# Alignment and feed-forward on one core: the tokens loaded once as tiles of 128 in a row, and their statistics moved between quadrants by small matmuls

## The reference, cut to what matters

```python
x = x + align(ctx_1024, layernorm(x))        # x (8, 512, 256), ctx (8, 64, 256), all float32
x = x + ffn(layernorm(x), w1, b1, w2, b2)    # 256 -> 1024 -> 256, quantised to 8 bits
# align, for each of the 8 batches, small = ctx (64 rows), large = tokens (512 rows):
D = sqrt(max(|a|^2 + |b|^2 - 2 a.b, 0))                        # 64 x 512
R[i, j] = D[i, j] + min(R[i-1, j], R[i, j-1], R[i-1, j-1])     # dynamic time warping
# backtrack the cheapest path from (63, 511) to (0, 0); expanded[j] += small[i] on the path
# ffn: h = relu(quant(quant(x) @ quant(w1).T + quant(b1))); out = quant(h) @ quant(w2).T + quant(b2)
```

## Time and profile before

| | us |
|---|---|
| median of 3 runs (205.34 to 207.87) | 205.64 |
| profiled execution, whole | 205.88 |
| its span, first to last instruction | 204.1 |
| first `to_chunks` starts | 44.16 |
| busy DVE / PE / ACT / POOL | 154.2 / 105.5 / 99.4 / 20.1 |

### The profile page before, as it was taken

How to read it: one execution, slowest core, us unless ns; L and a number is a source line. 1 busy time by engine, 2 the same in 40 slices (tenths; PEclk the granted TensorE clock), 3 DMA queues, 4 the chain that set the end, 5 groups by cost and what they waited for, 6 DMA issues and landing times.

```text
span 204.1 us, 3699 instructions
## 1 busy us (share of the span) xinstructions
PE 105.5 (52%) x1219; PEld 70.3 (34%) x1219; DVE 154.2 (76%) x743; ACT 99.4 (49%) x169; POOL 20.1 (10%) x81
## 2 busy tenths in 40 slices
PE   0089199100070000000000856699999999997993
PEld 0078199100040000000000322266565656564672
DVE  0566823999999999999999188586969696967342
ACT  0567039699992000021440005767576758566740
POOL 6455832300000000000000000000000000000000
PEclk9999859955555555555555699999999999999999
DMA  5999301999500000001103321001111113030214
GB/s 165 230 230 234 71 3 19 351 360 348 166 5 0 0 2 0 0 0 66 64 0 115 62 37 19 0 3 51 51 56 51 67 41 103 0 108 4 99 64 141
DMA packets 20597, 17.28 MB, mean 85 GB/s; under 512 B 6369, under 2 KB 20194, under 8 KB 20450
## 3 DMA queue, kind: packets, MB, share of 16 engines
q1 hardware_dynamic: 17986, 15.71, 26.5%
q10 hardware_dynamic: 2592, 1.34, 3.1%
HBM read 11.54 MB, written 5.51 MB: 84 GB/s over the span
## 4 chain that ended last, share of the span: by engine, by line
DVE 56%; PE 22%; ACT 10%; issue 6%; DMA 3%; SPq 1%; DVEq 0%; ACTq 0%
DVE Y L916 5%; DVE R L745 5%; PE y L1065 5%; ACT h_int L566 5%; DVE Dm L865 4%; PE h L1051 4%; DVE stats L848 4%; DVE X L843 4%; DMA X<-in_x_dram 3%; ACT M L560 3%; DVE A L713 3%; DVE enter L903 3%; DVE bcarry L902 3%; PE e L983 3%; DVE carry L733 3%
## 5 line engine op out<-in xcount | busy, mean ns | idle before, releaser
L566 ACT ACTIVATE h_int<-h,b_s 128x512 int16<-128x512 f32 x64 | 43.0, 685 | 8.6 <-PE h L1051 7.7
L1051 PE MATMUL h<-M,w1T 128*128 128x512 bf16 x128 | 37.9, 381 | 2.5 <-ACT h_int L566 1.7
L1065 PE MATMUL y<-w2T,XT 128*128 128x256 bf16 x256 | 37.7, 273 | 0.3 <-DVE XT L878 0.3
L1078 PE MATMUL y<-w1T 128*128 128x512 bf16 x19 | 5.9, 463 | 51.6 <-DVE S_lo L930 51.6
L1065 PEld LDWEIGHTS y<-w2T,XT 128*128 128x128 bf16 x256 | 25.0, 98 | 12.4 <-DVE XT L878 0.5
L878 DVE TENSOR_SCALAR XT<-h_int 128x1024 bf16<-128x1024 int16 x32 | 13.2, 424 | 18.3 <-ACT h_int L566 18.3
L1078 PEld LDWEIGHTS y<-w1T 128*128 128x128 bf16 x19 | 2.0, 116 | 54.6 <-DVE S_lo L930 51.9
L572 ACT ACTIVATE code<-Y,shifts 128x640 bf16<-128x640 bf16 x3 | 2.5, 828 | 37.5 <-DVE enter L903 37.5
L1020 PE MATMUL t<-ident_bf,w_raw 128*128 128x128 bf16 x32 | 4.6, 311 | 20.4 <-ACT w_raw L530 19.2
L689 DVE BATCH_NORM_STATS2 stats<-X 128x6 f32<-128x256 f32 x32 | 10.8, 410 | 4.1 <-DMA X<-in_x_dram 4.1
L843 DVE TENSOR_TENSOR X<-e,X 128x512 f32<-128x512 f32 x16 | 10.2, 682 | 4.6 <-PE e L1031 4.6
(11 more groups left out here) (165 smaller groups left out, 240.2 us busy)
## 6 DMA issues: line engine op xcount, KB each, us to landing
X<-in_x_dram SPq DMA_DIRECT2D x8, 512.0 KB, 8.9
out_dram<-E SPq DMA_DIRECT2D x32, 128.0 KB, 1.8
X<-in_x_dram SPq DMA_DIRECT2D x24, 128.0 KB, 9.6
w_raw<-in_L_ffn_w_dram SPq DMA_DIRECT2D x2, 1024.0 KB
X<-in_x_dram ACTq DMA_DIRECT2D x8, 128.0 KB, 7.3
S<-in_ctx_dram SPq DMA_DIRECT2D x1, 512.0 KB, 4.7
path_dram<-A SPq DMA_DIRECT2D x3, 160.0 KB, 1.8
path_dram<-XT SPq DMA_DIRECT2D x3, 160.0 KB, 1.9
```

Source lines behind the costliest of these rows:

```text
L566: nc.scalar.activation(h_int[:, g % 2, n, :], bank01[n % 2][:, :], ACT.Identity, bias=b1_s[:, n:n + 1], scale=1.0 / W_ONE).then_inc(h_roun ...
L1051: mm = nc.tensor.matmul(bank01[n % 2][:, :], w1T[:, k, n * P:n * P + P], xqT[:, g % 2, k, :], start=(k == 0), stop=(k == KH - 1))
L1065: mm = nc.tensor.matmul(bank67[t // 2][:, t % 2, :], hq[:, g % 2, n, t * P:t * P + P], w2T[:, n, :], start=False, stop=(n == NH - 1))
```

## The change

- The tokens come as eight transfers of 512 KB, all by SP, each of 128 partitions: tile (k, b) is the 128 tokens in a row from 128 k of batch b. They stay in SBUF; the second load is gone.
- `dots` takes for the quadrant of pair q the tiles 2q and 2q + 1 and, for a = 0 to 3, the columns 32 a to 32 a + 31 of the transposed tile. It waits for all turns of its load.
- The statistics of a token now stand in the partition of its place in 128, and are wanted at 32 q + lane. `spread_of` ends in `spread_parts`, the sum of squares masked by the token's quarter (`quarter`), and `spread_rows` on PE multiplies by a 0/1 matrix (`lane`): four matmuls per load, into a corner of a free PSUM bank. ACT reads that twice: the root (`std`) and a copy (`spread_sum`) for POOL's lengths. DVE makes `quarter` and `lane` by two reductions at the start.
- `norms` and `mirrored` have a buffer for each load and lie with `S_r1` in `h_int`, so `distances` waits for no `roots`.
- The orders change: PE runs a load of turns ahead of the dots; ACT makes `S_hi` before `Sc`, and `S_mid` after all roots; DVE takes the moments of three loads before the first `scales`; POOL no longer waits for the context's mean before its masks, and makes `S_r1` before the first `spread_of`.
- The weights are issued when the last dots are done, instead of after the last turn.

The diff, cut to its core:

```diff
-        def load_x(queue, k, h):
-            u0 = tile_of(k, CL * h)
-            for q in range(NQ):
-                queue.dma_start(X[TW * q:TW * q + TW, u0:u0 + CL, :],
-                                x_v[q, h, :, CL * k:CL * k + CL, :]).then_inc(x_in[k], 16)
+        def load_x(queue, k, a):
+            queue.dma_start(X[:, tile_of(k, B // 2 * a):tile_of(k, B // 2 * a) + B // 2, :],
+                            tiles_in[:, B // 2 * a:B // 2 * a + B // 2, k, :]).then_inc(x_in[k][a], 16)
...
+        def spread_bank(k):
+            bank_of = dist_banks[LOADS - 1 if k < LOADS - 1 else 0]
+            return bank_of[:, :, :].rearrange("p a b -> p (a b)")[:, UL * k:UL * k + UL]
...
-            sp.wait_ge(xT_done, LOADS * UL // 2)
+            sp.wait_ge(dot_done, LOADS)
...
-            sp.wait_ge(moments_made, NU)
-            for g in range(NG):
-                b, c = batch_of(g, 0), quad_of(g)
-                sp.dma_start(X[:, 4 * g:4 * g + 4, :], tiles_in[:, b:b + 4, c, :]).then_inc(x_again[g], 16)
...
-                nc.gpsimd.tensor_scalar(var_eps[:, us], centred_sum[:, us], 1.0 / D, EPS, ALU.mult,
-                                        ALU.add).then_inc(var_ready, 1)
+                nc.gpsimd.tensor_tensor(spread_parts[:, k, :, :], centred_sum[:, us].unsqueeze(2).to_broadcast([P, B, NQ]),
+                                        quarter[:, :].unsqueeze(1).to_broadcast([P, B, NQ]), ALU.mult).then_inc(parts_ready, 1)
...
             def spread(k):
-                act.wait_ge(var_ready, k + 1)
-                nc.scalar.activation(std[:, UL * k:UL * k + UL], var_eps[:, UL * k:UL * k + UL], ACT.Sqrt).then_inc(std_ready, 1)
+                act.wait_ge(spread_done, k + 1)
+                nc.scalar.activation(std[:, UL * k:UL * k + UL], spread_bank(k), ACT.Sqrt, bias=shifts[:, eps_at:eps_at + 1],
+                                     scale=1.0 / D).then_inc(std_ready, 1)
+                nc.scalar.activation(spread_sum[:, UL * k:UL * k + UL], spread_bank(k), ACT.Copy).then_inc(sum_copied, 1)
...
+            def spread_rows(k):
+                pe.wait_ge(parts_ready, k + 1)
+                if k == LOADS - 1:
+                    pe.wait_ge(prods_made, 1)
+                for q in range(NQ):
+                    mm = nc.tensor.matmul(spread_bank(k)[TW * q:TW * q + TW, :], lane[:, :],
+                                          spread_parts[:, k, 2 * q:2 * q + 2, :].rearrange("p h a -> p (h a)"),
+                                          start=True, stop=True)
+                mm.then_inc(spread_done, 1)
...
+            turns(0)
+            turns(1)
+            dots(0)
+            spread_rows(0)
+            turns(2)
+            dots(1)
+            spread_rows(1)
+            turns(3)
+            spread_rows(2)
+            dots(2)
+            spread_rows(3)
+            dots(3)
```

More of the change, by code:

```diff
@@ L186, in align_ffn_kernel @@
         h_int = sb("h_int", [P, 2, NH, 4 * P], i16)
+        early = h_int[:, :, :, :].rearrange("p a n t -> p (a n t)").bitcast(f32)
+        S_r1 = early[:, 0:NQ * D].rearrange("p (q d) -> p q d", d=D)
+        norms = early[:, NQ * D:NQ * D + LOADS * UL * I].rearrange("p (k u i) -> p k u i", k=LOADS, i=I)
+        mirrored = early[:, NQ * D + LOADS * UL * I:NQ * D + LOADS * UL * (I + HR)].rearrange(
+            "p (k u i) -> p k u i", k=LOADS, i=HR)
         hq = XT[:, :, :, :, :].rearrange("p a u k d -> p (a u k d)").bitcast(bf16).rearrange(
@@ L199, in align_ffn_kernel @@
         turn_banks = [bank01[0], bank01[1], flat4.bitcast(f32), bank5]
-        x_in = [sem(f"x_in{k}") for k in range(LOADS)]
+        x_in = [[sem(f"x_in{k}{a}") for a in range(2)] for k in range(LOADS)]
         ctx_loaded = sem("ctx_loaded")
@@ L213, in align_ffn_kernel @@
         lengths_made = sem("lengths_made")
-        x_again = [sem(f"x_again{g}") for g in range(NG)]
         path_out = [sem(f"path_out{p}") for p in range(len(PIECE_AT))]
@@ L305, in _ @@
             for k in range(LOADS):
-                load_x(sp, k, 0)
-                if k >= ACT_LOADS:
-                    load_x(sp, k, 1)
-            sp.wait_ge(xT_done, LOADS * UL // 2)
+                for a in range(2):
+                    load_x(sp, k, a)
+            sp.wait_ge(dot_done, LOADS)
             sp.dma_start(w1_raw[:, :, :], w1.rearrange("(p n) d -> p n d", n=NH)).then_inc(w_loaded, 16)
@@ L431, in token_lengths @@
                     ALU.add).then_inc(lengths_made, 1)
+            pool.wait_ge(ctx_split, 1)
+            nc.gpsimd.tensor_tensor(S_r1[:, :, :], S[:, :, :], S_hi[:, :, :], ALU.subtract).then_inc(ctx_rest, 1)
             spread_of(0)
-            pool.wait_ge(ctx_split, 1)
-            pool.wait_ge(ctxT_done, 2)
-            nc.gpsimd.tensor_tensor(S_r1[:, :, :], S[:, :, :], S_hi[:, :, :], ALU.subtract).then_inc(ctx_rest, 1)
             for k in range(1, LOADS):
@@ L473, in copy_xT @@
                                      turn_banks[n % 4][:, :], ACT.Copy).then_inc(xT_copied, 1)
+            act.wait_ge(ctx_loaded, 16)
+            nc.scalar.activation(S_hi[:, :, :], S[:, :, :], ACT.Copy).then_inc(ctx_split, 1)
             act.wait_ge(ctx_mean, 1)
@@ L494, in _ @@
                 copy_xT(0, j)
-            nc.scalar.activation(S_hi[:, :, :], S[:, :, :], ACT.Copy).then_inc(ctx_split, 1)
+            for j in range(UL // 2):
+                copy_xT(1, j)
             spread(0)
             for j in range(UL // 2):
-                copy_xT(1, j)
+                copy_xT(2, j)
             spread(1)
+            roots(0)
             for j in range(UL // 2):
-                copy_xT(2, j)
+                copy_xT(3, j)
+            spread(2)
+            for k in range(1, LOADS):
+                roots(k)
             act.wait_ge(ctx_rest, 1)
             nc.scalar.activation(S_mid[:, :, :], S_r1[:, :, :], ACT.Copy).then_inc(ctx_split, 1)
[L504 to L510, removed]
             act.wait_ge(w_loaded, 64)
@@ L758, in _ @@
             load_moments(1)
+            load_moments(2)
             scales(0)
-            load_moments(2)
-            scales(1)
             distances(0)
             load_moments(3)
[L764 to L768, removed]
+            for k in range(1, LOADS):
+                scales(k)
+                distances(k)
             masks()
```

85 lines of the change are left out of this document (48 added, 37 removed).

## The result

| | before | changed |
|---|---|---|
| median, us (4 runs each, on the same chip) | 205.62 (205.34 to 207.87) | 198.24 (197.38 to 198.68) |
| profiled execution, and its span | 205.88, 204.1 | 198.22, 196.4 |
| first `to_chunks` | 44.16 | 35.30 |
| from there to the end of the span | 159.9 | 161.1 |

The ratio is 0.9648 (95% interval 0.9609 to 0.9688): faster by 3.5%, where 196.0 had been forecast and 194.2 to 200.6 given as the range. The front gave 8.86 us; 1.2 of it were lost again in the later part.

A forecast was written before the change was run, and what follows sets the result against it. The first `to_chunks`, at 44.16, was the bound, behind a relay with a PE stop and 230 GB/s transfers. Moving it to 33.7 saves 10.4, less 0.7 for handovers is 9.7: 196.0 us, range 194.2 to 200.6.

The forecast's parts named there:

- 1. `S` lands, the load ends: Context and token transfers: `S` alone at first, 349 GB/s; lands at 4.6 against 5.48, last bytes move near 15.7.
- 5. first dots; first `rstd`: First load on PE, ACT and DVE: dots take 1.99, 14.1 to 16.1; after `spread_rows` and root, `rstd` at 16.6.
- 6. first shuffle ends; second distances end: DVE: 2.87 from `rstd` to shuffle's end at 19.5; fourth load's moments to 22.2, second distances to 25.1.
- step 7: PE's second dots: missing program block, held until the load ends, there at 18.6; 0.2 us lost instead of 4.17.
- 8. root of load 2 ends; third distances end: ACT after the second dots: root of load 2 at 25.05, tying with DVE free at 25.1; third distances 28.0.
- step 9: Fourth load (load 3): POOL's lengths and spread, then last dots end at 27.8 and fourth distances at 30.9.
- 10. masks; `to_chunks`: End of the front: 2.79 from shuffle's end to `to_chunks`, at 33.7 against 44.16; last roots hidden.
- The costs set at nothing: Removing the second load gives nothing; later weights, `S_mid`'s new place, the two reductions and SP's queue cost nothing.
- rival A: PE's stop comes again in full, PE resuming at 22.7; saves 4.0 to 5, about 201 us; chance 0.10.
- the 0.7 given back: Front: 0.7 us taken off the 10.4 saved, for new handovers between PE and ACT, leaving 9.7.
- What stands behind it moves with it: Everything after the first `to_chunks` shifts with it; 160 us from there to the end, as before.
- a sign of being wrong: The forecast is wrong if PE stops long in the second dots, first dots start after 16, or those 160 us change.

The follow-up runs named there:

- e1: Changed kernel plus 32 tiny float32 matmuls at the head of PE's program; 200.72 us, ratio 0.9935 to the kernel before.
- e3: Changed kernel with each token transfer cut into four of 32 partitions, same bytes and order; 203.71 us, ratio 1.006 to the kernel before.
- e4: Changed kernel with the second token load (eight 512 KB transfers and their waits) put back behind the weights; 198.28 us, ratio 0.9828 to the kernel before.
- e2: Changed kernel without the second half of the contraction in the dots of loads 2 and 3, distances not the reference's; 198.63 us.
- e8: e7 with the masks made in two halves in other gaps of DVE; 195.35 us, ratio 0.9557 to the kernel before.
- e10: e8 with seven instead of ten warm-up matmuls ahead of the feed-forward stage's align matmuls; 194.06 us, ratio 0.9591 to the kernel before.
- e5: The changed kernel itself, unchanged, timed again on a second chip; 198.24 us, ratio 0.9674 to the kernel before.
- e7: Changed kernel with 22 PE records fewer: context lengths in one matmul, `spread_rows` for two loads at a time; 194.65 us, ratio 0.953 to the kernel before.

## Why the prediction was right, and where it was off

The timetable, step by step:

| step | forecast | measured |
|---|---|---|
| 1. `S` lands, the load ends | 4.6, 15.7 | 4.65, 16.0 |
| 5. first dots; first `rstd` | 14.1 to 16.1; 16.6 | 13.86 to 15.85; 16.31 |
| 6. first shuffle ends; second distances end | 19.5; 25.1 | 19.46; 25.06 |
| 7. PE has the block; second dots end | 18.6; 20.3 | 18.71; 20.5 |
| 8. root of load 2 ends; third distances end | 25.05; 28.0 | 24.6; 28.7 |
| 9. last dots end; fourth distances end | 27.8; 30.9 | 30.5; 32.5 |
| 10. masks; `to_chunks` | 2.79; 33.7 | 2.80; 35.30 |
| behind it | 159.9 | 161.1 |

**Right:** the whole relay up to 25 us, within 0.5 at each point and mostly 0.3. Above all step 7, on which the sum rests: the stop is a program block, held until the load is over. It was read from three rows of before, and e1 and e3 bear it out by moving first the record and then the load's end. In the changed kernel itself the hold hardly mattered: PE entered the block before at 14.5 and went on 4.2 later, where a block asked for with the DMA idle took 3.5 to 4.1. Without any hold step 7 would have come to nearly the same, so its small stop is no evidence for the hold; the kernel before, e1 and e3 are. The costs set at nothing were nothing (e4 for the reload; 67.8 from `to_chunks` to `S_lo`, as before, for the later weights and `S_mid`), and so rival A, the stop in full, had its answer: the stop came again at 4.11 where the load lasted as long (e3), at 2.90 where the block was asked for earlier in the short load (e1), and else was under 0.5.

**Off, in the front:** 0.9 later than the 34.4 that I took, which is 33.7 and the 0.7 given back. Step 7 counted one block. But PE needs one every 127 matmul records or so, and as the rows after show a block takes 3.5 to 4.1 us from entering one to entering the next, while 127 records of this shape run in 2.0. So once the dots stand close together PE starves at every block. The earlier trace rows had the pace and the earlier trace rows the count of packets, and e2 prices the term at 1.1. It failed at step 9's last dots, 2.7 late. The rest is as allowed: DVE takes 3.0 from one `rstd` to the next and not 2.87, and POOL, which makes `spread_of(3)` ahead of the third load's lengths, is some 0.35 late with them; together 0.8, which e2 shows by itself: 17.89 from `rstd` to `to_chunks` without the late stops, where the forecast had 17.1. That it nearly equals the 0.7 given back is luck, as those were for handovers between PE and ACT. The first `rstd` was 0.3 early. 33.7 - 0.3 + 1.1 + 0.8 = 35.3.

**Off, behind the front:** 1.2. "What stands behind it moves with it" is true for 67.8 us, up to `S_lo`. Then 0.9 goes to warm-up matmuls at half clock, whose pace hangs on when the clock rises, and that was 2.0 later here (e8 to e10). Since it rose at another moment again in e5, the same kernel, nothing shows that the change made it later. The other 0.3 lies behind the first add and stays open. The forecast had no term for it, and listed it as a sign of being wrong.

Both together, 2.0 (0.84, since 9.7 less than 44.16 is 34.46, and 1.2), are what lies between 196.2, the forecast by the profiled execution, and the 198.22 measured.

**Row and rule.** The measured stops settle what was left open. The program packets on q8 are 16 KB, ten of them in the execution, and the stop stands at the same record whatever the time; but PE takes 3.5 to 4.1 us a block where its instructions would run in 2.0, and more when the token load is running. The Trainium skill, page "Runtime: NRT & Kernel Launch", section "Instruction fetch mechanics", states blocks of 16 KiB and 256 instructions, and says that the next one is fetched while the current one runs, mostly hidden. The size agrees with the packets, and the count with the 127 matmul records, which with a weight load each are 254; hidden it is not in this front. The Trainium skill, page "DMA: Bandwidth & Descriptors", section "Queues, rings and completion order", says that each DMA engine switches between queues packet by packet. The 8 KB packet at 20.2 us agrees with that. PE's does not: in the three kernels in which a block was asked for well before the load's end (before at 16.6, e1 at 12.0, e3 at 16.7), its packet went when the token queue ran dry, at 21.9, 15.9 and 22.3, and not earlier. The measurement decides for the wait of PE's blocks.

## What to carry to other kernels

An "issue" gap on PE that ends 2 to 3 us after a 16 KB packet on the instruction queue is, as far as these runs show, a missing program block. It moves with the number of instructions ahead of it and, here, with the end of the token load, so wide transfers and fewer matmuls both shortened it (e3 backwards, and e7). Count blocks for the whole dense stretch, not only up to the first stop. A fixed number of warm-up matmuls ahead of critical work costs their time at the low clock: take as many as fit before the data lands, and no more.

## What the runs showed of the hardware

- 32-partition transfers ran at 227 to 230 GB/s, 128-partition ones at 349; the narrow and smaller ones cost e3 6.3 us in the front.
- A program block of 127 fp32 matmul records took 3.54, 4.10 and 3.64 us with the DMA idle but for the packet, the packet 1.1 to 1.3 after PE had entered the block before. At 15.5 ns a record the matmuls take 2.0.
- PE's 16 KB program packet did not pass the running token load: the block before was entered near 12.0 in e1 and the packet went at 15.9; 16.6 and 21.9 in the kernel before, 16.7 and 22.3 in e3. An 8 KB packet on the other instruction queue did pass it, at 20.2 in the kernel before.
- The clock rose 2.8 us after `S_lo` in one kernel, 4.8 in the next and 5.9 in the next one's repeat, on the same warm-up matmuls after 47 to 52 us of idleness. From `to_chunks` to the end those two executions of one kernel took 161.1 and 163.3, so a difference of 1 or 2 us between two kernels can be no more than that.
